# Local attention values as pairs of chunks: 36 columns per matmul instead of 72 with accumulation

## The reference, cut to what matters

```python
attn = softmax(einsum('bhqd,bhkd->bhqk', q, k) * SCALE)      # within one chunk
out  = einsum('bhqk,bhkd->bhqd', attn, v)
local_out  = chunks of 16 neighbouring tokens
atrous_out = chunks of 16 tokens that lie 3 apart            # dilation 3
return linear(local_out + atrous_out, Wo, bo)
```

## Time and profile before

| | us |
|---|---|
| median of 3 runs | 403.94 |
| lowest, highest | 402.14, 410.02 |
| the profiled execution | 407.52 |
| its span | 405.7 |

### The profile page before, as it was taken

One profiled execution on the slowest core, in us unless ns is written; L12 is line 12 of the kernel. 1 busy time (PEld: TensorE's weight loads), 2 busy tenths in 40 slices (PEclk: granted clock), 3 DMA queues, 4 the chain that ended last, 5 costly groups with the idle time before them and its releaser, 6 DMA issues.

```text
span 405.7 us, 11513 instructions
## 1 busy us (share of the span) xinstructions
PE 352.9 (87%) x4472; PEld 210.3 (52%) x4472; DVE 288.0 (71%) x720; ACT 210.6 (52%) x458; POOL 123.2 (30%) x149
## 2 busy tenths in 40 slices
PE   6856997989899999689988968898899999979995
PEld 5433544555546555255644635555446665546563
DVE  6779489886678789566889877876434475766853
ACT  6264314645644566356355554644756555625553
POOL 6177433150312330260425000000021354535443
PEclk9995799999999999899999999998999999989999
DMA  7252031223210323111221330132000000000000
GB/s 197 55 164 62 2 97 26 77 66 70 89 33 2 95 80 61 22 32 67 43 78 28 63 70 13 39 89 72 3 2 0 0 2 26 2 28 0 27 0 26
DMA packets 27476, 19.34 MB, mean 48 GB/s; under 512 B 12120, under 2 KB 25816, under 8 KB 27384
## 3 DMA queue, kind: packets, MB, share of 16 engines
q1 hardware_dynamic: 27208, 18.42, 18.4%
q10 hardware_dynamic: 216, 0.20, 0.2%
HBM read 6.81 MB, written 3.70 MB: 26 GB/s over the span
## 4 chain that ended last, share of the span: by engine, by line
PE 46%; SPq 17%; DVE 17%; POOL 6%; issue 6%; ACT 4%; DMA 2%; DVEq 0%; ACTq 0%; POOLq 0%
PE bank_B L1403 11%; SPq L613 8%; SPq L537 6%; PE bank_c L1307 6%; PE bank_A L1409 5%; PE bank_B L1211 5%; PE bank_A L1349 3%; DVE neg_max L1043 3%; PE bank_M L1372 2%; PE bank_M L1252 2%; ACT p_mla L865 2%; SPq L619 2%; PE bank_M L1357 1%; PE bank_M L1247 1%; DVE s_loc L1060 1%
## 5 line engine op out<-in xcount | busy, mean ns | idle before, releaser
L865 ACT ACTIVATE p_mla<-bank_B 128x512 f32<-128x512 f32 (+1 forms) x176 | 95.6, 561 | 78.2 <-PE bank_B L1197 77.4
L1043 DVE TENSOR_REDUCE neg_max<-bank_A 128x1 f32<-128x512 f32 (+3 forms) x176 | 109.1, 637 | 30.2 <-PE bank_A L1197 27.0
L1211 PE MATMUL bank_B<-q_stack,k_stack 54*128 54x512 bf16 (+3 forms) x256 | 63.0, 304 | 15.5 <-DVE neg_max L1043 7.5
L1190 PE MATMUL bank_A<-k_stack,q_stack 52*128 52x512 bf16 (+3 forms) x256 | 65.3, 312 | 4.5 <-DVE neg_max L1043 3.4
L1403 PE MATMUL bank_B<-xrT,k_diag 128*128 128x512 f32 x128 | 63.1, 613 | 1.3 <-DVE k_diag L1168 1.3
L747 POOL TENSOR_TENSOR x<-x,q_part 128x512 f32<-128x512 f32 x31 | 39.5, 1274 | 57.4 <-ACT q_part L899 50.2
L1307 PE MATMUL bank_c<-p_mla,v_mla 128*32 128x128 f32 (+12 forms) x512 | 47.9, 447 | 2.9 <-ACT p_mla L865 2.8
L1211 PEld LDWEIGHTS bank_B<-q_stack,k_stack 54*128 54x128 bf16 x256 | 19.3, 94 | 57.7 <-issue 31.1
L899 ACT ACTIVATE q_part<-bank_A,expert_w 128x128 f32<-128x128 f32 x108 | 30.8, 368 | 30.1 <-PE bank_A L1409 30.1
L1197 PE MATMUL bank_A<-masks 64*128 64x64 bf16 (+2 forms) x352 | 44.5, 206 | 0.0
L1197 PE MATMUL bank_B<-masks 64*128 64x64 bf16 (+2 forms) x352 | 43.4, 202 | 0.7 <-issue 0.7
(11 more groups left out here) (148 smaller groups left out, 541.4 us busy)
## 6 DMA issues: line engine op xcount, KB each, us to landing
k_stack<-parts SPq DMA_DIRECT2D x48, 64.0 KB
q_stack<-parts SPq DMA_DIRECT2D x45, 64.0 KB
v_dram<-v_rows SPq DMA_DIRECT2D x4, 648.0 KB, 3.3
k_diag<-k_part SPq DMA_DIRECT2D x48, 34.0 KB
v_diag<-v_dram SPq DMA_DIRECT2D x32, 45.0 KB, 2.0
v_diag<-v_dram SPq DMA_DIRECT2D x32, 36.0 KB, 2.0
x<-in_x SPq DMA_DIRECT2D x4, 256.0 KB, 8.4
out<-x SPq DMA_DIRECT2D x3, 256.0 KB, 2.2
```

What stands on the lines that cost most here:

```text
L865: drained_by(nc.scalar.activation(p_of(n)[:, m:m + len(heads), 0:w], src, ACT.Exp, scale=SCALE), step)
L1043: drained_by(nc.vector.tensor_reduce(neg_max[:, g, m:m + len(heads), i], src, AX.X, ALU.max, negate=True), step)
L1190: return nc.tensor.matmul(bank_of(step)[:, n * w:(n + 1) * w], q_stack[b % 2][rows, h % 8, i * P:(i + 1) * P], k_stack[b % 2][rows, h % 8, ...
L1211: nc.tensor.matmul(bank_of(step)[:, m * w:(m + 1) * w], k_stack[b % 2][rows, h % 8, j * P:(j + 1) * P], q_stack[b % 2][rows, h % 8, j * P: ...
```

## The change: what it does

A matmul of LO holds four heads of both chunks of a pair, where it held eight heads of one chunk. The 128 rows of contraction are now two chunks x four heads x 16 keys. So each matmul has 4x9 = 36 columns and is complete by itself; `par` becomes `s`, which counts the halves of the heads. The number of matmuls is the same.

For this `v_diag` is laid out as [4 heads, 2 halves, 4 pairs, ...], and each load takes 16 DMAs (2 chunks x 4 heads x 2 halves) of four runs for each partition, instead of 8 DMAs of eight runs. ScalarE's copies in PT become six per unit: for each half of the partitions, one of 256 elements and two of 128 (in a full unit). The mask of the heads depends on the half of the partitions, so `k_diag` for batch 0 is written one half at a time (two instructions for one), and for the other batches the DMAs go to other places of `k_diag`.

```diff
-    heads = (np.arange(P)[:, None] // HD % X == np.arange(X)).astype(np.float32)
+    row, of, place = np.arange(P)[:, None, None], np.arange(2)[None, :, None], np.arange(X)[None, None, :]
+    heads = (row // HD % X == (place + X // 2 * (of ^ row // SLOT)) % X).astype(np.float32)
...
-        v_diag = sb("v_diag", [P, X, 8, QUADS - LOCAL_QUADS, VX])
+        v_diag = sb("v_diag", [P, X // 2, 2, 4, QUADS - LOCAL_QUADS, VX])
...
-                    for g in range(X):
-                        sp.dma_start(v_diag[CHUNK * g:CHUNK * g + CHUNK, g, :, 0:i1 - i0, :].rearrange("k q i c -> k q (i c)"),
-                                     v_dram[b, :, g, i0:i1, :].rearrange("(q k) i c -> k q (i c)", k=CHUNK)).then_inc(v_diag_in, 16)
+                    of = v_dram[b, :, :, i0:i1, :].rearrange("(j t k) x i c -> t x k j (i c)", t=2, k=CHUNK)
+                    for top in range(2):
+                        for x_ in range(X // 2):
+                            rows = slice(SLOT * top + CHUNK * x_, SLOT * top + CHUNK * x_ + CHUNK)
+                            for s in range(2):
+                                sp.dma_start(v_diag[rows, x_, s, :, 0:i1 - i0, :].rearrange("k j i c -> k j (i c)"),
+                                             of[s ^ top, x_ + X // 2 * s]).then_inc(v_diag_in, 16)
...
-                            sp.dma_start(k_diag[rows, :, x_, :], k_part[rows]).then_inc(k_diag_in, 16)
+                            places = [(x_ + X // 2 * (a ^ top)) % X for a in range(2)]
+                            sp.dma_start(view(k_diag[rows, 0, places[0], :],
+                                              ((X + places[1] - places[0]) * PAIRS * CHUNK, 2), (1, PAIRS * CHUNK)),
+                                         k_part[rows]).then_inc(k_diag_in, 16)
...
-                        nc.scalar.activation(k_diag[:, :, x, :], k_part[:], ACT.Copy,
-                                             scale=head_mask[:, x:x + 1]).then_inc(k_diag_by_act, 1)
+                        for a in range(2):
+                            ins = nc.scalar.activation(k_diag[:, a, x, :], k_part[:, a, :], ACT.Copy,
+                                                       scale=head_mask[:, a, x:x + 1])
+                        ins.then_inc(k_diag_by_act, 1)
...
-                    for par in range(2):
-                        ins = nc.scalar.copy(view(pT_loc[:, t % PT_RING, par, 0, CHUNK * par:], (P, n), (PAIR, np_), (1, CHUNK)),
-                                             view(bank[:, CHUNK * par:], (P, n), (PAIR, np_), (1, CHUNK)))
+                    for top in range(2):
+                        rows = slice(SLOT * top, SLOT * top + SLOT)
+                        to = pT_loc[rows, t % PT_RING]
+                        nc.scalar.copy(view(to[:, top, 0, 0:], (P, 2 * tiles), (PAIR, np_), (1, CHUNK)),
+                                       view(bank[rows, 0:], (P, 2 * tiles), (PAIR, np_), (1, CHUNK)))
+                        for g in range(2):
+                            ins = nc.scalar.copy(
+                                view(to[:, 1 - top, g, CHUNK:], (2 * P, tiles), (PAIR, np_), (1, CHUNK)),
+                                view(bank[rows, P * (1 - g) + CHUNK:], (2 * P, tiles), (PAIR, np_), (1, CHUNK)))
...
-                    pe.wait_ge(v_diag_in, 16 * X * (2 * b + segment + 1))
-                    w = X * (HD + 1)
+                    pe.wait_ge(v_diag_in, 16 * 2 * X * (2 * b + segment + 1))
+                    w = X // 2 * (HD + 1)
                     for i in range(loc_tiles(step)):
                         for g in range(2):
-                            c = 2 * w * i + w * g
-                            for par in range(2):
+                            for s in range(2):
+                                c = 4 * w * i + 2 * w * g + w * s
                                 for j in range(min(4, len(LUNITS[step[2]][0]) - 4 * i)):
-                                    of_chunk = v_diag[:, :, 2 * j + par, 2 * step[2] + i - SEGMENTS[segment][0], :]
+                                    of_pair = v_diag[:, :, s, j, 2 * step[2] + i - SEGMENTS[segment][0], :]
                                     last = nc.tensor.matmul(bank[PAIR * j:PAIR * j + PAIR, c:c + w],
-                                                            pT_loc[:, t % PT_RING, par, 2 * i + (g ^ par), PAIR * j:PAIR * j + PAIR],
-                                                            of_chunk[:, :, (HD + 1) * g:(HD + 1) * g + HD + 1],
-                                                            start=par == 0, stop=par == 1, skip_group_check=True)
+                                                            pT_loc[:, t % PT_RING, s, 2 * i + g, PAIR * j:PAIR * j + PAIR],
+                                                            of_pair[:, :, (HD + 1) * g:(HD + 1) * g + HD + 1],
+                                                            start=True, stop=True, skip_group_check=True)
```

More of the change, by code:

```diff
@@ L401, in build @@
         k_part = sb("k_part", [P, 2, PAIRS * CHUNK])
-        head_mask = sb("head_mask", [P, X])
+        head_mask = sb("head_mask", [P, 2, X])
         k_diag = sb("k_diag", [P, 2, X, PAIRS * CHUNK])
         v_rows = sb("v_rows", [P, X, QUADS, VX])
-        v_diag = sb("v_diag", [P, X, 8, QUADS - LOCAL_QUADS, VX])
+        v_diag = sb("v_diag", [P, X // 2, 2, 4, QUADS - LOCAL_QUADS, VX])
         pT_loc = sb("pT_loc", [P, PT_RING, 2, 4, P])
@@ L766, in _ @@
         def _(act):
-            nc.scalar.memzero(v_diag[:].rearrange("p x q i c -> p (x q i c)")).then_inc(v_zeroed, 1)
+            nc.scalar.memzero(v_diag[:].rearrange("p x s j i c -> p (x s j i c)")).then_inc(v_zeroed, 1)
             act.wait_ge(wide_in, 16)
@@ L840, in _ @@
                 elif kind == "PT":
-                    t, np_, n = loc_no(step), loc_rows(step) // PAIR, 2 * loc_tiles(step)
+                    t, np_, tiles = loc_no(step), loc_rows(step) // PAIR, loc_tiles(step)
                     act.wait_ge(pT_cleared, 1)
@@ L1034, in _ @@
                     if n < KD_FIRST:
-                        nc.vector.tensor_scalar(k_diag[:, :, n, :], k_part[:], head_mask[:, n:n + 1], None,
-                                                ALU.mult).then_inc(k_diag_by_dve, 1)
+                        for a in range(2):
+                            ins = nc.vector.tensor_scalar(k_diag[:, a, n, :], k_part[:, a, :], head_mask[:, a, n:n + 1],
+                                                          None, ALU.mult)
+                        ins.then_inc(k_diag_by_dve, 1)
                 elif kind == "S":
```

## The result

| | before | after |
|---|---|---|
| median of the runs, us | 406.56 (4 runs) | 422.43 (4 runs) |
| lowest to highest | 402.14 to 410.02 | 419.86 to 424.44 |
| profiled execution, its span | 407.52, 405.7 | 424.36, 422.2 |
| mean granted clock | 0.964 | 0.929 |

The change makes the kernel slower: the ratio is 1.045, with a 95% interval of 1.033 to 1.056. All ratios compare undisturbed executions alone, so a median of all runs may lie beside its ratio; it does so most in the changed kernel with 8 issues and four copies, where 4 of 12 executions are counted. The forecast of 412.9 us was too low, and the time lies above its range, while the sign was right.

A forecast was written before the change was run, and what follows sets the result against it. No engine alone bounded it: TensorE held 46% of the chain, SP's queue 17%. Batches 0 to 3 and the clock, 1.5+2.95-0.5+3.8+1.2 = +9.0 us on a median of 403.94, gave 412.9; 8-in-10 range 402.5 to 417.5.

The forecast's parts named there:

- ScalarE's cost: PT step: six copies instead of two, +0.67 us per full unit, mostly covered; 0.67 charged once, at batch 1's unit 1.
- the largest term: SP's queue: each v_diag load issues 16 DMAs instead of 8, +3.84 us per load, landing 2.0 us after its last issue.
- the clock: TensorE in batch 3, after its longer wait for v_diag: a stretch at lower granted clock, charged 1.2 us.
- Its lower price: SP's queue: lower bound for a v_diag load's additional issues, 8x0.24 = +1.9 us instead of +3.84.
- an issue that costs by its runs: Rival at SP's eight v_diag loads: only +1.9 us a load, so 405 us, within 2%; chance 0.20.
- Batch 0: Second v_diag load lands late: LO of unit 2 waits 2.0 us and is 0.5 shorter, +1.5 us.
- Batch 1: Second load starts 0.15 us later, queue gap absorbs only 1.0 of 3.84: shift copy TensorE awaits +2.95 us later.
- Batch 2: Both v_diag loads have room and one LO is on the chain: -0.5 us.
- Batch 3: First load on the chain +3.84 us, second +2.2, less what the shorter LO units give back: +3.8 in sum.
- LO: TensorE's local value matmuls: 36 columns instead of 72, 0.65 us per full unit instead of 1.17, 0.52 saved.
- Shorter matmuls that win: Rival on TensorE: all units give their gain, loads cost little, 399 us (403 with half the gain); chance 0.14.
- A floor under them: Rival on TensorE: pitch stops falling between 72 and 36 columns; 414.8 us with half the gain, 416.7 with none; chance 0.15.

The follow-up runs named there:

- again: The changed kernel measured once more, unaltered, in a later set against the kernel before: 418.32 us, ratio 1.032.

## Why the prediction was wrong

The step that failed is ScalarE's cost: "most of this is covered", +0.67 us, where six copies alone cost 4.7. Beside it the base was 2.6 us too low, and by the ratio of the first result the loads cost more than their term. The mechanism of the largest term, the queue of SP with late landings, was the one forecast. The working below uses 13.1 us for the change (ratio 1.032) and 18.2 (ratio 1.045), the two measurements that there are; by the medians they are 12.3 and 15.9.

**The base.** The forecast was set on a median of 403.94; beside the changed kernel the same program had 406.56. That is 2.6 of the 9.5 us by which 422.43 lies above 412.9. The copies are 4.0 more; the 2.9 that are left fall to the loads and to what the two measurements of the same kernel differ by.

**The copies: the term that failed.** The prediction charged +0.67, one unit, and left 12 us of ScalarE "covered". The length was right (1.32 predicted, 1.40 measured), the cover was not: six copies alone cost 4.7 us, four 2.2. The prediction named the mechanism (a transpose needs the PSUM bank that the copy empties) and then applied it to one place of the chain of before; the same chain has a pair at 134.74 as well, and in 50 to 110 us one at 71.61. For the exponentials behind the copies it trusted in the three banks B, but the wait for them rose from 2.8 to 5.4 us with six copies alone, and to 5.7 in the changed kernel. That a wait of 0.65 us is not in the chain says that it is shorter than its cover, not that the cover is 1.3 us long. In batch 0 the chain of before ran for the most part through SP's queue; the copies pulled it over to TensorE and ScalarE. The Trainium skill (TensorEngine Tiling (Array Packing), PSUM Bottleneck) says that tiling (one array used as several small ones) speeds up TensorE but not the copy out of PSUM, which may then become the bottleneck. This case is a neighbour of that one: the copies cost 4.7 us with TensorE's matmuls left as they were, because there were more of them.

**The loads.** Predicted +12.0 in all (2.0, 2.8, 3.84 and 2.2, with 1.2 of the clock). Measured: 11.9 (1.032 less 1.003) or 17.0 (1.045 less 1.003) inside the changed kernel, and 17.1 (12.6 to 21.5) alone. So the term is right by the first and 5 us too low by the others. Its price per load was low in any case: the mean of the eight loads rose from 4.22 us to 8.50, +4.28 instead of +3.84. The pieces of the chain show what the sum missed (changed kernel):

```profile
142.07 1.65 SPq L588
...
251.35 1.67 SPq L588
...
256.81 1.76 DMA v_diag<-v_dram
```

Seven of the eight loads of 16 hold one issue of 1.1 to 1.7 us among others of 0.43. Before, three of the eight loads held one. The prediction took the load at 67.52, which had none, as the unit price for all. And it has no term for the first load of batch 0, although TensorE waits 1.5 us for it in both executions, ahead of unit 0, where it did not wait before. Its lower price, "8x0.24 = +1.9", does not follow from its own rule: 16 issues of 0.24 us are the old 3.84, so an issue that costs by its runs would have made the load no longer at all. The rows exclude both.

**Stage by stage**, by the start of the same issue in SP's queue less that of the earlier trace rows (the first load, which is not among those rows, started at 51.04):

| start before | predicted | changed | again |
|---|---|---|---|
| load, 51.04 | 0 | -0.7 | -1.4 |
| shift, 80.23 | +1.5 | +3.6 | +1.1 |
| shift, 104.04 | +1.5 | +3.2 | +0.7 |
| load, 131.39 | +1.7 | +4.7 | +2.2 |
| shift, 144.10 | +4.5 | +8.7 | +6.0 |
| load, 239.78 | +4.0 | +8.7 | +6.1 |
| load, 255.15 | +8.0 | +13.6 | +10.9 |
| span | +9.0 | +16.5 | +10.2 |

- Batch 0: +1.5 lies between what the two executions show (3.2 and 0.7), and that is luck: in the four kernels here that differ from the one before only in loads or copies, the first load starts anywhere from 48.5 to 51.7 us. Counted from the second load to the shift copies behind it, 12.7 us became 15.4 and 15.0: +2.7 and +2.3 for the forecast's +1.5, since that load took 8.9 and 8.6 us, not 7.7. The wait of unit 2 was 1.72 us, predicted 2.0. Whether the wait for the first load reaches the end is not shown: in one execution the second load then starts 18.1 us after the first, in the other 16.7, and 16.5 before.
- Batch 1 failed in both: 5.5 and 5.2 us between 104.04 and 144.10, predicted 2.95. A part of the excess is the load (+4.95 and +4.46 us instead of 3.84), the larger one its start, 1.5 later instead of 0.15. That lateness goes with the copies: in the kernel before with six copies and loads of 8 issues the same load starts 29.3 us after the shift copy of batch 0, where it was 27.4. The wait for the shift copies at 174.70 grew from 3.6 to 5.0.
- Batch 2: nothing, predicted -0.5.
- Batch 3: 4.9 and 4.7 from 239.78 to 255.15, predicted 4.0 with the clock. TensorE waited 4.8 and 3.5 us ahead of unit 0 (predicted 5.3), and the clock behind it was low, as expected: in the changed kernel 258 to 262 us ran at a granted clock of 0.50. The last stage, from 255.15 to the end, is +2.9 in one execution and -0.7 in the other, predicted +1.0.

**LO.** 0.70 us per unit instead of the predicted 0.65, so 0.47 saved instead of 0.52. The line through two widths held nearly. That the sum came out at 3.6 us, for 3.8 predicted, is in part luck: its interval reaches from 0 to 7. The Trainium skill (TensorEngine Tiling (Array Packing), Instruction Overhead) says that a matmul with one column lasts as long as one with 60; read as a floor of 60 columns, it would make the unit about 1.0 us, an estimate. The trace does not agree: 0.70.

**The rivals.** An issue that costs by its runs is excluded: DMAs of half the runs took 8.5 us per 16, and splitting without any other edit cost as much. Shorter matmuls that win are excluded. A floor under them is excluded by 0.70 us a unit. What was missing among the cases was one above the forecast in which more of the copies are uncovered and nearly every load holds a long issue: the prediction named both upper ends, 12 us of uncovered copies and 5.2 us per load, but the first did not reach into its range, and with the second it stopped at 417.5.

## What to carry to other kernels

Count DMA issues in a queue that is in order, before bytes or runs: here 8 issues per load fitted into the slack and 4 fewer won nothing, while 8 more cost 3 to 4%. When an instruction gets longer, its cover has to be measured at each of its occurrences, by the next user of the buffer that it frees, by the user of the data that it makes, and by the instructions behind it on its own engine. And a price per instruction is a mean over all its instances with the long ones in it, not that of a clean one.

## What the runs showed of the hardware that was not expected

- For fp32 matmuls with 32 columns of weights, 64 recorded instructions with 36 moving columns take 0.70 us up to the next matmul's start, 10.9 ns each, against 18.3 ns at 72 columns and 31 ns at 128.
- SP's DMA issues of v_diag last 0.43 us, and about one in 17 of them lasts 1.0 to 2.0 us (80 of 1340 in the profiles here), with loads of 8 as of 16; what causes it was not tried.
- A ScalarE copy of 64x256 elements takes as long as one of 128x256 (0.37 us), so splitting by partitions doubles its time: four copies of 64 rows took 1.28 us, two of 128 rows 0.65 us.
- The same program's two profiled spans differ by 6.3 us with the clock over 40 to 300 us at 0.92 and 0.96. A single profile of such a kernel places a stage no better than that.
